# Level masks on GpSimd, ten chunks by updates, a shared LayerNorm and an earlier score chain in a two-layer transformer kernel

## The reference

```python
x = norm(x + attention(x))       # 16 heads of 64, rotary, window of 32, softmax
x = norm(x + ffn(x))             # 128 -> 512 -> 128, relu
x = norm(x + delta_block(x))     # below
x = norm(x + routed_ffn(x))      # light FFN for all tokens, heavy one for 128 of them
# delta_block, per sequence
q, k, v = split(ln(x) @ gates_w + gates_b); lr = ln(x) @ lr_w + lr_b
k = k / norm(k)
A = tril(k @ k.T, -1) + I
u = solve_triangular(A, v)
y = (q @ k.T) @ (lr * u)
x = x + y @ out_w + out_b
x = x + relu(ln(x) @ w1 + b1) @ w2 + b2
# routed_ffn
s = x @ routing_token
50 times: a = log(k) - logsumexp(s + b); b = -relu(s + a)    # the descent
heavy FFN where exp(s + a + b) is among the top 128
```

## Time and profile before

| | us |
|---|---|
| three executions | 460.81, 466.7, 483.89 (median 466.7) |
| the profiled execution | 466.78 |
| its span in the profile | 465.0 |
| TensorE busy, weight load busy | 406.5, 357.1 |
| VectorE, ScalarE, GpSimd busy | 324.6, 254.4, 168.2 |

### The profile page before, as it was taken

The page is one execution under the profiler, slowest core; times in us unless marked ns, Lnnn a source line. Parts: engine busy times, 40 slices in busy tenths (PEclk is TensorE's granted clock), DMA queues, the critical chain, the costliest instruction groups (busy, mean ns, idle before and its releaser), DMA issues.

```text
span 465.0 us, 18396 instructions
## 1 busy us (share of the span) xinstructions
PE 406.5 (87%) x7464; PEld 357.1 (77%) x7464; DVE 324.6 (70%) x1583; ACT 254.4 (55%) x669; POOL 168.2 (36%) x192
## 2 busy tenths in 40 slices
...
DMA packets 20515, 35.34 MB, mean 76 GB/s; under 512 B 4368, under 2 KB 11536, under 8 KB 20432
## 3 DMA queue, kind: packets, MB, share of 16 engines
...
## 4 chain that ended last, share of the span: by engine, by line
PE 52%; DVE 16%; SPq 11%; ACT 7%; issue 5%; DMA 5%; POOL 4%; DVEq 0%; ACTq 0%; POOLq 0%
PE QK L523 7%; SPq L448 6%; PE VY L596 4%; DMA t_swap<-t_sin 4%; PE O L680 3%; PE O L574 3%; PE S L551 3%; POOL qk L1601 2%; PE QK L747 2%; PE O L751 2%; DVE unread_tests L1267 2%; DVE t_sin L965 2%; PE PT L560 2%; PE PT L583 2%; PE S L778 2%
## 5 line engine op out<-in xcount | busy, mean ns | idle before, releaser
L1601 POOL TENSOR_TENSOR qk<-t_cos,t_swap 128x512 f32<-128x512 f32 x64 | 80.5, 1280 | 104.1 <-DMA t_swap<-t_sin 100.5
L1358 ACT ACTIVATE probs<-probs,negative_max 128x64 f32<-128x64 f32 x256 | 67.9, 339 | 44.0 <-DVE negative_max L974 44.0
L965 DVE TENSOR_TENSOR t_cos<-QK,cos 128x512 f32<-128x512 f32 x64 | 44.0, 688 | 32.6 <-POOL qk L1601 21.3
L1633 POOL TENSOR_TENSOR rstd<-var_eps,minus_half 128x4 f32<-128x4 f32 x24 | 25.4, 1058 | 101.2 <-DVE var_eps L1037 81.4
L965 DVE TENSOR_TENSOR t_sin<-QK,sin 128x512 f32<-128x512 f32 x64 | 43.5, 680 | 0.0
L974 DVE CUSTOM_DVE_ANT_0 probs<-S,masks 128x64 f32<-128x64 f32 x256 | 39.2, 217 | 6.1 <-PE S L551 5.8
L523 PE MATMUL QK<-xnT,wq 128*128 128x128 f32 x256 | 36.3, 287 | 2.6 <-DVE t_sin L965 1.9
L1373 ACT COPY v_own<-VY 128x512 f32<-128x512 f32 x32 | 18.8, 587 | 35.9 <-PE VY L539 35.9
L596 PE MATMUL VY<-wo,oT 128*128 128x128 f32 x256 | 36.8, 287 | 0.7 <-ACT oT L1379 0.7
L523 PEld LDWEIGHTS QK<-xnT,wq 128*128 128x128 f32 x256 | 32.8, 201 | 3.9 <-DVE t_sin L965 2.3
L523 PE MATMUL QK<-xnT,wk 128*128 128x128 f32 x256 | 35.5, 283 | 0.1
...
## 6 DMA issues: line engine op xcount, KB each, us to landing
...
```

The source lines that it names most:

```text
L965: last = nc.vector.tensor_tensor(dst[:, u % G, PAIRS * j:PAIRS * j + PAIRS], QK[j][:].rearrange("p (m t) -> p m t", m=PAIRS), table[:, tok ...
L1358: last = nc.scalar.activation(probs[:, u % G, m, e, :], probs[:, u % G, m, e, :], ACT.Exp, scale=-1.0, bias=negative_max[:, u % G, e, m:m ...
L1601: nc.gpsimd.tensor_tensor(qk[:, h, c, WINDOW:WINDOW + P], t_cos[:, h, c], t_swap[:, h, c], ALU.add).then_inc(rope_done, 1)
L1633: nc.gpsimd.tensor_tensor(rstd[:, grp(q)], var_eps[:, grp(q)], minus_half[:, grp(q)], ALU.pow).then_inc(roots_done, 1)
```

## The change

Five things change.

1. The ten level masks are made by GpSimd, behind the same `gram` copies, and `invert_pairs` has no mask in it; each of its products waits for itself (`chained`).
2. Chunks 0 to 9 (`NU`) take an update form: keys are corrected in transposed form four chunks ahead, the value correction is accumulated with the negated key correction times the state, VectorE copies that update, and keys times update are accumulated as the state, which VectorE copies. Chunks 10 to 15 keep corrections and transitions, which `prepare` makes between the steps of the chain. Banks change.
3. In the delta LayerNorm ScalarE standardises groups 0 and 1, with a shift that GpSimd makes of VectorE's negated mean; VectorE standardises groups 2 and 3 behind the statistics of all. Forty products `warm` are issued ahead of the transposes, and `mlp_base` stands elsewhere in GpSimd's list.
4. The transpose of the score ends, the last two `scaled` groups and the exponentials stand ahead of the FFN pieces.
5. Six pieces are issued ahead of the descent in place of twelve.

The diff, cut (semaphores, tiles, the removed corrections and transitions loops, and ScalarE's three small copy functions, which are the old loop bodies with new banks, are left out):

```diff
+    NU = 10
+    NM = NB - NU
...
-    BEFORE_DESCENT = 12
+    BEFORE_DESCENT = 6
...
+            def correct_keys(n):
+                if n % GB == 0:
+                    pe.wait_ge(inverses_updated, 2 * NLEV + n // NH + 1)
+                    wait(pe, key_corrections_kept, n // GB)
+                last = nc.tensor.matmul(B[0][:, tok(n % GB)], kv[:, n, 0:C], invT[:, n, :], start=True, stop=True)
+                if n % GB == GB - 1 or n == NU - 1:
+                    last.then_inc(key_corrections_ps, 1)
+            def correct_values(n):
+                wait(pe, updates_of_chunk_kept, n - 1)
+                pe.wait_ge(inverses_updated, 2 * NLEV + n // NH + 1)
+                last = nc.tensor.matmul(B[6 - 2 * (n % 2)][:, 0:C], invT[:, n, :], kv[:, n, C:2 * C], start=True, stop=(n == 0),
+                                        skip_group_check=True)
+                if n == 0:
+                    last.then_inc(updates_of_chunk_ps, 1)
+            def weighted_sum(n):
+                nc.tensor.matmul(B[3][:, 0:C], weighted_keys[:, n, :], updates[:, n, :], start=(n == 0), stop=False,
+                                 skip_group_check=True)
+            def correct_both(n):
+                m, i = (n - NU) // 2, (n - NU) % 2
+                if i == 0:
+                    wait(pe, corrections_kept, m)
+                last = nc.tensor.matmul(B[1][:, 256 * i:256 * i + 256], invT[:, n, :], kv[:, n, 0:2 * C], start=True, stop=True)
+                if i == 1:
+                    last.then_inc(corrections_ps, 1)
+            def find_transition(n):
+                m, i = (n - NU) // 2, (n - NU) % 2
+                if i == 0:
+                    pe.wait_ge(corrections_kept, m + 1)
+                    wait(pe, transitions_kept, m)
+                nc.tensor.matmul(B[2][:, 256 * i:256 * i + C], corrections[:, n - NU, 0:C], kv[:, n, 0:C], start=True, stop=True)
+                last = nc.tensor.matmul(B[2][:, 256 * i + C:256 * i + 256], corrections[:, n - NU, 0:C], weighted_keys[:, n, :],
+                                        start=True, stop=True)
+                if i == 1:
+                    last.then_inc(transitions_ps, 1)
+            def prepare(k):
+                n = NU + k // 4 * 2 + k % 2
+                if k % 4 < 2:
+                    correct_both(n)
+                else:
+                    find_transition(n)
+            correct_values(0)
+            for n in range(GB):
+                correct_keys(n)
+            correct_values(1)
+            pe.wait_ge(weighted_keys_done, TG)
+            pe.wait_ge(inverses_updated, 2 * NLEV + 2)
+            for n in range(NU):
+                if n > 0:
+                    pe.wait_ge(key_corrections_kept, n // GB + 1)
+                    pe.wait_ge(state_kept, n)
+                    nc.tensor.matmul(B[6 - 2 * (n % 2)][:, 0:C], minus_corrections_T[:, n, :], state[:, n, :], start=False, stop=True,
+                                     skip_group_check=True).then_inc(updates_of_chunk_ps, 1)
+                    weighted_sum(n - 1)
+                if n + GB < NU:
+                    correct_keys(n + GB)
+                pe.wait_ge(updates_of_chunk_kept, n + 1)
+                nc.tensor.matmul(B[5][:, 0:C], kv[:, n, 0:C], updates[:, n, :], start=(n == 0), stop=True,
+                                 skip_group_check=True).then_inc(state_ps, 1)
+                if 1 < n + 1 < NU:
+                    correct_values(n + 1)
+                prepare(n)
+            weighted_sum(NU - 1)
+            for n in range(NU, NB):
+                m = n - NU
+                last = nc.tensor.matmul(B[3][:, 0:C], weighted_keys[:, n, :], corrections[:, m, C:], start=False, stop=False,
                                         skip_group_check=True)
                 if n < NB - 1:
                     wait(pe, state_kept, n - 1)
-                    last = nc.tensor.matmul(B[5 + n % 2][:, 0:C], kv[:, n, 0:C], corrections[:, n, C:], start=True, stop=(n == 0),
+                    last = nc.tensor.matmul(B[7 - 2 * (m % 2)][:, 0:C], kv[:, n, 0:C], corrections[:, m, C:], start=True, stop=False,
                                             skip_group_check=True)
-                if n > 0:
-                    pe.wait_ge(transitions_kept, n // 2 + 1)
-                    pe.wait_ge(state_kept, n)
-                if 0 < n < NB - 1:
-                    last = nc.tensor.matmul(B[5 + n % 2][:, 0:C], transitions[:, n, 0:C], state[:, n, :], start=False, stop=True,
-                                            skip_group_check=True)
+                pe.wait_ge(transitions_kept, m // 2 + 1)
+                pe.wait_ge(state_kept, n)
                 if n < NB - 1:
-                    last.then_inc(state_ps, 1)
-                if n > 0:
-                    last = nc.tensor.matmul(B[7][:, 0:C], transitions[:, n, C:], state[:, n, :], start=False, stop=(n == NB - 1),
-                                            skip_group_check=True)
+                    nc.tensor.matmul(B[7 - 2 * (m % 2)][:, 0:C], transitions[:, m, 0:C], state[:, n, :], start=False, stop=True,
+                                     skip_group_check=True).then_inc(state_ps, 1)
+                last = nc.tensor.matmul(B[3][:, 0:C], transitions[:, m, C:], state[:, n, :], start=False, stop=(n == NB - 1),
+                                        skip_group_check=True)
+                if NU + m < 2 * NM:
+                    prepare(NU + m)
...
+            warm(40, 2)
             for s in range(TG + 2):
                 if s < TG:
-                    to_channels(3, s, lambda n: XB[:, n, :], mn_tokens_ready, s + 1)
+                    to_channels(3, s, lambda n: XB[:, n, :], *((mn_tokens_ready, s + 1) if s < 2 else (later_mn_tokens_ready, s - 1)))
...
             warm(28)
-            ffn_pieces(range(6, PIECES_EACH))
             pe.wait_ge(ends_reduced, 2)
             nc.tensor.transpose(B[6][0:2, 0:P], ends[:], ident[:]).then_inc(endsT_ps, 1)
             warm(8)
             pe.wait_ge(ends_diagonal_done, 1)
             nc.tensor.matmul(B[6][:, 0:2], ones[0:2, :], ends_diagonal[:], start=True, stop=True).then_inc(ends_ps, 1)
             x3_to_channels(3)
-            ffn_pieces(range(PIECES_EACH, BEFORE_DESCENT))
-            warm(8)
+            warm(16)
...
-                nc.vector.tensor_tensor(quarters_T[:, l, n], gram[:, n], masked(l), ALU.mult).then_inc(quarters_masked, 1)
...
-                nc.vector.tensor_tensor(squares_inv[:, n], gram[:, n], masked(NLEV + 1), ALU.mult).then_inc(dve_step, 1)
-                nc.vector.tensor_tensor(squares_invT[:, n], gram[:, n], masked(NLEV), ALU.mult).then_inc(dve_step, 1)
-                mask_quarters(0, i)
-                count[0] += 2
-                dve.wait_ge(dve_step, count[0])
-                for t in (squares_inv, squares_invT):
+                for t, m in ((squares_inv, NLEV + 1), (squares_invT, NLEV)):
+                    chained(nc.vector.tensor_tensor(t[:, n], gram[:, n], masked(m), ALU.mult))
                     nc.vector.tensor_tensor(t[:, n], t[:, n], masked(NLEV + 2), ALU.add).then_inc(pairs_inverted, 1)
 
...
-                dve.wait_ge(state_ps, n + 1)
-                if n == 0:
-                    last = nc.vector.tensor_copy(state[:, 1, :], B[5][:, 0:C])
+                if n < NU:
+                    dve.wait_ge(updates_of_chunk_ps, n + 1)
+                    nc.vector.tensor_copy(updates[:, n, :], B[6 - 2 * (n % 2)][:, 0:C]).then_inc(updates_of_chunk_kept, 1)
+                    dve.wait_ge(state_ps, n + 1)
+                    nc.vector.tensor_copy(state[:, n + 1, :], B[5][:, 0:C]).then_inc(state_kept, 1)
                 else:
+                    dve.wait_ge(state_ps, n + 1)
                     dve.wait_ge(state_kept, n)
-                    last = nc.vector.tensor_tensor(state[:, n + 1, :], state[:, n, :], B[5 + n % 2][:, 0:C], ALU.add)
-                last.then_inc(state_kept, 1)
+                    nc.vector.tensor_tensor(state[:, n + 1, :], state[:, n, :], B[7 - 2 * ((n - NU) % 2)][:, 0:C], ALU.add).then_inc(state_kept, 1)
             dve.wait_ge(g_ps, 1)
-            nc.vector.tensor_copy(g_matrix[:], B[7][:, 0:C]).then_inc(g_kept, 1)
...
-                if q >= 1:
-                    standardise(XB, XD, q - 1, mn_tokens_ready)
-            standardise(XB, XD, TG - 1, mn_tokens_ready)
+                if q < 2:
+                    nc.vector.tensor_scalar(minus_mean[:, grp(q)], mean_var[:, grp(q), 0], -1.0, None, ALU.mult).then_inc(delta_mean_out, 1)
+            for q in range(2, TG):
+                standardise(XB, XD, q, later_mn_tokens_ready)
 
...
+            keep_key_corrections(0)
+            keep_corrections(0)
+            keep_key_corrections(1)
+            keep_transitions(0)
+            keep_key_corrections(2)
+            keep_corrections(1)
+            keep_transitions(1)
+            keep_corrections(2)
+            keep_transitions(2)
...
+            def standardised(q):
```

(41 more changed lines are left out.)

67 lines of the change are left out of this document (24 added, 43 removed).

## The result

| kernel | executions | median, us | span, mean granted clock of the profiled one |
|---|---|---|---|
| before, at first | 4 | 470.4 (460.8 to 483.9) | 465.0 us, 0.977 |
| after | 4 | 476.15 (475.1 to 476.6) | 474.2 us, 0.946 |

The ratio after to before is 1.026, 95% interval 1.015 to 1.038: slower, clear of the noise, though the interval leaves open whether by over 2%. Between the two profiled executions it is 9.3 us, where +3.6 was forecast. One thing has to be known for all that follows: executions of the kernel before come in two kinds, some at a mean granted clock of 0.97 to 0.98 and some at 0.91 to 0.96, and the ratios, which leave disturbed executions out, are mostly against the first kind.

What follows compares the result with a forecast made beforehand. The prediction saw a mix, TensorE holding half the chain of waits, VectorE 16%, no engine the bound everywhere. Masks +2.6, chain -2.9, LayerNorm +0.8, score and descent +3.1 gave +3.6 on 466.78: 470.4 us, eight in ten within 461 to 475.

Steps and rivals of the forecast that it cites:

- Masks, +2.6: Start of the inversions: masks on GpSimd delay TensorE's first product of the second half by 2.6 us.
- The turns of one operation: Pair inversions: GpSimd masks and VectorE operations from SBUF alternate, one operation each, making the first product 2.6 us later.
- Chain, -2.9: Corrections and chain of states: ten chunks by updates save 2.9 us, at 1.86 us a chunk.
- the allowance of 0.2: Chain of states: 0.2 us taken off a 3.1 us gain, as the second link holds 0.92 us work in 0.93.
- The rival of the low clock in this place: Chain of states: the new chain drops TensorE to 1.2 GHz, 482 us in all; chance 0.08.
- LayerNorm, +0.8: Delta LayerNorm: sharing standardisation with ScalarE costs 0.8 us, bounds -0.1 and +1.7.
- Score start, -0.2: Score ends to first partial: moving them early gains only 0.2 us, as GpSimd's adds hold VectorE's operations.
- Descent, +3.3: First to last partial: six more pieces and gelu waits add 3.3 us, 49 us for 45.87.
- Tail, 0: Last partial to the end: no difference forecast, 0 us.
- 1 + 1 - 0.8: Descent: gelu waits of about 1 us at pieces 18 and 38, less one 0.8 us wait that goes; booked as +1.0.
- The base: Whole kernel before: profiled execution of 466.78 us and median of 466.7 taken as the same starting time.
- The third rival: Chain of states: TensorE falls to 1.2 GHz, nine chunks give 12 us, 482 us in all; chance 0.08.

Runs made afterwards that it cites:

- u_masks: The changed kernel with the ten level masks back on VectorE; median 474.9 us.
- u_norm: The changed kernel with the delta LayerNorm on VectorE alone and without its 40 warming products; median 478.0 us.
- score_only: The kernel before with only score ends, exponentials and gelus early and six pieces ahead of the descent for twelve; median 478.8 us, ratio 1.017.
- masks_gated: The changed kernel with level 0 masks back on VectorE and levels 1 to 4 on GpSimd behind the last pair inverse; median 474.8 us.
- warm_stall: The changed kernel with 24 more warming products directly ahead of piece 18, where TensorE waits for a gelu; median 474.3 us.
- warm_both: The changed kernel with 24 warming products ahead of piece 18 and 34 ahead of the places' product behind the descent; median 473.4 us.
- gated_warm_tail: The kernel before with update chunks, level 1 to 4 masks on GpSimd behind the last pair inverse, and 34 and 44 warming products in the tail's gaps; 462.6 us.
- after_warmed: The changed kernel with warming products in the descent's odd iterations, the tail's gaps and ahead of pieces 18 and 38; 471.3 us.
- u_score: The changed kernel with score ends, exponentials, gelus and the twelve pieces ahead of the descent as before; median 475.0 us.
- chain_only: The kernel before with the ten chunks by updates alone; 461.9, 462.4, 471.7 and 478.3 us, ratio 0.997.
- chain_gated: The kernel before with the ten chunks by updates and level 1 to 4 masks on GpSimd behind the last pair inverse; median 464.5 us, ratio 0.996.
- before_warmed: The kernel before with three warming products per odd descent iteration and 34 and 44 in the tail's gaps; 466.9 us, ratio 1.000.
- warm_counts: As gated_warm_tail, plus three warming products in each odd iteration of the descent; median 461.6 us, ratio 0.982 to the kernel before.

## Why the prediction was wrong

It had the sign and, but for the clock, nearly the size: +3.6 forecast, +4.5 between the two kernels that keep the clock. The time came out at 476, above the range of 461 to 475, because the forecast took the granted clock of the descent and of the tail as fixed, and its base as the kernel's usual time.

- **Masks, +2.6: right.** The turns of one operation, 8.2 us to the first product, and the relief where they are taken away are all shown. Over the profiles of this study, first mask to first correction took 41.0 us on average with all masks on GpSimd (eight profiles, 40.2 to 41.7) and 38.3 with none (six, 37.8 to 39.2): +2.7. Some of that is the clock: between profiles with 3.4 us of 1.2 GHz in this stage it is 40.2 against 38.1, +2.1. Of the Trainium skill ("SBUF — State Buffer", "Who interferes with whom") the trace bears out that VectorE operations with two SBUF inputs are held and that those from PSUM are not (0.67 us beside the same masks). `digit_widths`, one SBUF tile and a pointer, lasted 1.15 us beside an add; the section has that too, since it counts `tensor_scalar` among the operations that can take the shared ports.
- **Chain, -2.9: right in kind, 0.5 short.** All fourteen profiles with the part give 25.9 us to the copy of g, the four without it 29.4. A chunk took 1.81 us, not 1.86, and the allowance of 0.2 was not needed. The rival of the low clock in this place fell: clock 1.00 in each profile.
- **LayerNorm, +0.8: too small.** Shared: 32.5 to 34.0 us in nine profiles, mean 33.2; on VectorE alone 30.8 to 31.7 in nine others, mean 31.2; so +2.0, beyond the upper bound of 1.7. Some of it is the clock again: with 6.8 us of 1.2 GHz in the stage it is 33.0 against 31.15, +1.8. The four activations were taken at 0.32 us from a row with one pointer and lasted 0.41, so that the first transposes are 0.9 us late, not 0.5. VectorE's first addition came 1.1 us later than before (0.7 forecast) and the second 1.45 (1.1 forecast), and that lateness reaches the end of the stage whole; the forecast took 0.8 although its own working had come to 1.1.
- **Score start, -0.2: too small a gain**, -1.5 to -1.6 in each profile with the part. It had `digit` wait for the third add and the widths for the fourth; `digit` was not held, the widths were held by the third, and nothing up to the first partial was held by the fourth.
- **Descent, +3.3: the step that failed.** The waits at pieces 18 and 38 were foreseen (1 us each; 0.76 and 1.01 measured), but the cost of a wait was taken as its length. What the runs showed in its place: in all five profiles in which TensorE waits at piece 18 at full clock (the changed kernel twice, u_masks, u_norm, score_only), the clock falls 0.4 to 1.1 us behind the start of that wait and stays at 1.2 GHz for 14 to 24 us, in which a piece lasts 1.17 us for 0.65; in the three in which the wait is filled it does not fall there. The longer wait at piece 38 is followed by no fall in four of these five profiles (score_only does not have it; in masks_gated, warm_stall and warm_both one of 3.4 to 6.8 us comes two to five microseconds behind it), and gated_warm_tail falls at the same place without a wait, so the wait makes a fall likely and does not decide it alone. Of the +7.9, after_warmed keeps 5.8. In these lie 3.4 us of low clock and two groups of warming products, which last 1.2 us more than the waits that they fill (1.50 and 1.5 us against 0.76 and 1.01). Without them some 3 to 4.6 us are left, an estimate from these numbers that takes the low stretch at half its length or at nothing; the forecast's +3.3 lies in it, and the rest is the clock. Two slips in the term changed little: 1 + 1 - 0.8 is 1.2 and not 1.0, and the wait for a gelu that goes was 0.50 us in the trace before, not 0.8.
- **Tail, 0: missed.** Nothing in it was changed. Its +4.0 is the clock as well: with the gaps filled it takes 30.4 us before and 30.5 after. What puts more of the tail at 1.2 GHz in the changed kernel than in the kernel before is not shown; the waits at its two gaps are there in both.
- **The base.** The sum started from one execution, of 466.8 us at clock 0.977, and the median of three (466.7) seemed to confirm it. Over 69 executions the median is 471.7. That the median of three fell together with the profiled one was luck, and the spread of 460.8 to 483.9 in the same three was the sign that the profile showed one of two ways in which the kernel runs, and that a forecast from it holds for that way only. The third rival had the right mechanism, a fall of the clock behind a gap, in the wrong place: it looked for it in the chain, at 95% busy, and not at the waits that the score part adds.

Open: what starts a fall. u_score, chain_only, chain_gated and the kernel before fall at 31 to 33 us behind the first partial, where TensorE waits for nothing over 0.5 us, gated_warm_tail at 13.5 and masks_gated at 3. That filling slivers there ends it is shown by before_warmed (12 of 12) and warm_counts (6 of 6); how the chip decides is not.
